# Attention and mixture-of-experts layer: the normalised output turned by a crossbar DMA, and engine orders of their own for each half

## The reference

```
xn  = layernorm(x)
qkv = xn @ W_qkv                      # 32 query heads, 16 key/value heads, 64 wide
p   = softmax(q k^T / 8 + slope_h * (key - query), causal)
s   = concat_heads(p v) @ W_out       # 2048 -> 128
g   = silu(moe(xn))                   # 8 experts, top 2, gelu, 128 -> 512 -> 128
out = x + s * g
```

## Time and profile before

| what | us |
|---|---|
| median of 3 runs | 1367.28 (1366.29 to 1369.7) |
| the profiled execution's own time | 1373.28 |
| its span, first to last instruction | 1370.9 |
| PE / DVE / ACT / POOL busy | 1251.3 / 1103.1 / 891.0 / 833.9 |
| prologue, about | 0 to 90 |
| first half's bodies, about | 90 to 623 |
| experts' stage | 624 to 761 |
| second half's bodies, end of the program | 761 to 1350, 1371 |

### The profile page before, as it was taken

One profiled execution on the slowest core, in us unless ns is written; L12 is line 12 of the kernel. 1 busy time (PEld: TensorE's weight loads), 2 busy tenths in 40 slices (PEclk: granted clock), 3 DMA queues, 4 the chain that ended last, 5 costly groups with the idle time before them and its releaser, 6 DMA issues.

```text
span 1370.9 us, 53673 instructions
## 1 busy us (share of the span) xinstructions
PE 1251.3 (91%) x18202; PEld 934.0 (68%) x18203; DVE 1103.1 (80%) x3404; ACT 891.0 (65%) x1663; POOL 833.9 (61%) x1015
## 2 busy tenths in 40 slices
PE   1589999999999999988999799999999999999992
PEld 0357677777777777767888477766767777667762
DVE  8778788888888888856888688888888888878864
ACT  1367677777777777765666477667666666666662
POOL 7147677777777777780000177776666676666773
PEclk9789999999999999998999899999999999999996
DMA  7223333333333333322222233333333232333322
GB/s 263 89 64 90 77 86 87 87 89 86 84 84 84 84 84 84 84 64 66 80 80 73 70 79 79 78 77 72 71 75 74 69 73 70 72 74 77 77 55 65
DMA packets 113023, 112.37 MB, mean 82 GB/s; under 512 B 17250, under 2 KB 101570, under 8 KB 112324
## 3 DMA queue, kind: packets, MB, share of 16 engines
q1 hardware_dynamic: 108868, 103.18, 30.0%
q0 software_dynamic: 4096, 8.40, 2.0%
HBM read 18.91 MB, written 16.78 MB: 26 GB/s over the span
## 4 chain that ended last, share of the span: by engine, by line
PE 29%; POOL 14%; issue 6%; DVE 5%; ACT 1%; DVEq 0%; POOLq 0%; DMA 0%; SPq 0%; ACTq 0%
POOL h L609 10%; PE ps L631 4%; PE ps L632 4%; PE ps L633 4%; POOL y_now L601 3%; DVE stage L1112 2%; PE ps L728 2%; PE ps L703 2%; PE outs L759 2%; PE ps L732 1%; PE outs L631 1%; PE outs L632 1%; PE outs L633 1%; PE ps L772 1%; DVE mix L1181 1%
## 5 line engine op out<-in xcount | busy, mean ns | idle before, releaser
L609 POOL TENSOR_TENSOR h<-stage 128x512 f16<-128x512 f32 x640 | 646.2, 1038 | 422.1 <-ACT stage L961 384.6
L1112 DVE CUSTOM_DVE_ANT_0 stage<-ps,kmask 128x512 f32<-128x512 f32 (+3 forms) x1024 | 451.7, 488 | 138.4 <-PE ps L703 136.8
L961 ACT ACTIVATE stage<-ps,slope 128x512 f32<-128x512 f32 (+1 forms) x768 | 432.5, 616 | 84.7 <-PE ps L735 81.2
L728 PE MATMUL ps<-q_st,k_st 128*128 128x256 f16 (+3 forms) x1024 | 303.3, 302 | 7.2 <-ACT stage L961 6.3
L759 PE MATMUL outs<-v_sp,stage 128*128 128x65 f16 x2560 | 292.7, 195 | 15.6 <-POOL h L609 12.1
L950 ACT CAST q_st<-ps 1x512 f16<-1x512 f32 x256 | 147.9, 578 | 219.9 <-PE ps L711 218.4
L761 PE MATMUL outs<-v_sp,stage 128*128 128x64 f16 x2560 | 289.8, 194 | 0.0
L763 PE MATMUL outs<-v_sp,h 128*128 128x65 f16 x2560 | 288.9, 193 | 0.0
L759 PEld LDWEIGHTS outs<-v_sp,stage 128*128 128x128 bf16 x2560 | 234.5, 98 | 70.1 <-POOL h L609 33.2
L761 PEld LDWEIGHTS outs<-v_sp,stage 128*128 128x128 bf16 x2560 | 237.5, 98 | 0.0
L763 PEld LDWEIGHTS outs<-v_sp,h 128*128 128x128 f16 x2560 | 237.4, 99 | 0.0
(11 more groups left out here) (192 smaller groups left out, 2852.3 us busy)
## 6 DMA issues: line engine op xcount, KB each, us to landing
q_st<-q_raw SPq DMA_DIRECT2D x256, 128.0 KB, 2.4
k_st<-k_raw SPq DMA_DIRECT2D x128, 128.0 KB, 2.2
q_st<-q_raw SPq DMA_DIRECT2D x256, 64.0 KB, 2.0
k_st<-k_raw SPq DMA_DIRECT2D x128, 64.0 KB, 2.0
stage<-slot_x SPq DMA_DIRECT2D x40, 128.0 KB, 2.0
slot_y<-stage SPq DMA_DIRECT2D x40, 128.0 KB, 1.7
slot_x<-att SPq DMA_DIRECT2D x2, 2048.0 KB, 8.7
wx_raw<-in_L_ffn_w SPq DMA_DIRECT2D x64, 64.0 KB, 1.8
```

Source lines behind the costliest of these rows:

```text
L609: pool.tensor_tensor(t_lo[r], t_p[r], upper(t_p[r]), ALU.subtract).then_inc(s[f"lo{u % NG}"], 1)
L728: pe.matmul(d, k[:, 0, at], q[:, 0, seen], start=True, stop=False, skip_group_check=True)
L961: e = act.activation(t_p[r][:, c0:c1], S_ps[u % 2][:, c0:c1], ACT.Exp, scale=slope[:, bass.ds(pair_index(n) * 2 * SLOTS + sl * 2 + h, 1)])
L1112: ins = dve.tensor_tensor_reduce(junk[h][:, c0:c0 + w], M_ps[h][:, c0:c0 + w], kmask[:, SEQ - w:SEQ], 1.0, -3e38, ALU.add, ALU.max, mx[sl] ...
```

## The change

The A task no longer uses PE. ACT and DVE split a_sb (SBUF, fp32) into a new 16-bit buffer `a16` of 128 x 1024 (512 high columns, then 512 low), and SP turns the whole buffer with one crossbar DMA for each slot and body into `aT`, high and low together. `project` waits for that DMA instead of for `al`. A leaves the G banks. `a16` lies in the stage buffer where the experts' stage has its inputs and outputs, so SP waits for all transposes before the first expert load and ACT waits for the last expert store before the second half's main windows. `ORDER` and `G_USERS` become one set for each half, with the sends and fetches one window later (I and D at -2), A at -1 on DVE and SP, and one more window at the end of each half.

```diff
-    [("Q1", 1), ("A1", -1), ("O0", -1), ("K0", 2), ("A0", 0)],
-    [("V0", 1), ("Q0", 2)],
+    [   # the same for both halves
+        [("V0", 1), ("O0", -1)],
+        [("Q0", 1), ("Q1", 1), ("K0", 2)],
+    ],
...
+ORDER = [   # the second half's list; the first half's differs in places
+        "PE": [
+            ("P6", -1), ("Q0", 1), ("S0", 0), ("P7", -1), ("M5", 0), ("S1", 0), ("P8", -1), ("S2", 0), ("C1", 0),
+            ("S3", 0), ("P9", -1), ("V0", 1), ("M0", 1), ("Q1", 1), ("S4", 0), ("P0", 0), ("M1", 1), ("S5", 0),
+            ("S6", 0), ("P1", 0), ("P2", 0), ("M2", 1), ("S7", 0), ("S8", 0), ("P3", 0), ("C0", 1), ("P4", 0),
+            ("S9", 0), ("K0", 2), ("M3", 1), ("P5", 0), ("O0", -1), ("M4", 1),
+        ],
+        "DVE": [
+            ("O0", -2), ("B5", 0), ("A0", -1), ("Q0", 1), ("N1", -1), ("B0", 1), ("A1", -1), ("B1", 1), ("B2", 1),
+            ("F0", -2), ("F1", -2), ("Q1", 1), ("N0", 0), ("V0", 1), ("B3", 1), ("K0", 2), ("B4", 1),
+        ],
+        "POOL": [
+            ("I1", -2), ("L6", -1), ("D0", -2), ("L7", -1), ("L8", -1), ("L9", -1), ("D1", -2), ("L0", 0),
+            ("L1", 0), ("L2", 0), ("L3", 0), ("L4", 0), ("I0", -1), ("L5", 0),
+        ],
+        "SP": [   # first half: K1 +1, A0 -1, A1 -1, Q0 +1, W0 +2, Q1 +1, K0 +2
+            ("K1", 0), ("Q0", 0), ("K0", 1), ("Q1", 0), ("A0", -1), ("A1", -1),
+        ],
...
+        aT = [h_flat[:, s * 2 * SEQ:(s + 1) * 2 * SEQ] for s in range(SLOTS)]
+        a16 = [piece(8 + s).bitcast(F16) for s in range(SLOTS)]
...
+            def turn_out(n, _, sl):
+                sp.wait_ge(s[f"al{sl}"], n + 1)
+                need(sp, "op", n)
+                sp.dma_start_transpose(aT[sl].rearrange("p (t q) -> p t q", q=P), a16[sl]).then_inc(s[f"ta{sl}"], 16)
...
-                need(pe, f"nrm{sl}", n + 1)
-                bank_free(n, f"A{sl}")
-                for t in range(QT):
-                    mm = pe.transpose(bank_of[f"A{sl}"][:, t * P:(t + 1) * P], a_sb[sl][:, t, :], ident[:, :])
...
-                    need(pe, f"al{sl}", n + 1)
+                    need(pe, f"ta{sl}", (n + 1) * 16)
...
-                act.wait_ge(s[f"ta{sl}"], n + 1)
-                need(act, "op", n)
-                act.copy(aT_hi[sl], bank_of[f"A{sl}"][:, :]).then_inc(s[f"ah{sl}"], 1)
+                act.wait_ge(s[f"nrm{sl}"], n + 1)
+                need(act, f"ta{sl}", n * 16)
+                act.copy(a16[sl][:, 0:SEQ], a_sb[sl].rearrange("p t c -> p (t c)")).then_inc(s[f"ah{sl}"], 1)
...
-                dve.tensor_tensor(aT_lo[sl], bank_of[f"A{sl}"][:, :], aT_hi[sl], ALU.subtract)\
+                dve.tensor_tensor(a16[sl][:, SEQ:2 * SEQ], a_sb[sl].rearrange("p t c -> p (t c)"),
+                                  a16[sl][:, 0:SEQ], ALU.subtract).then_inc(s[f"al{sl}"], 1)
```

More of the change, by code:

```diff
@@ L194, in build @@
         h_flat = h_hi[:, :, :, :].rearrange("p r a b -> p (r a b)")
-        aT_hi = [h_flat[:, s * SEQ:(s + 1) * SEQ] for s in range(SLOTS)]
-        aT_lo = [h_flat[:, (SLOTS + s) * SEQ:(SLOTS + s + 1) * SEQ] for s in range(SLOTS)]
+        aT = [h_flat[:, s * 2 * SEQ:(s + 1) * 2 * SEQ] for s in range(SLOTS)]
+        aT_hi, aT_lo = ([m[:, part * SEQ:(part + 1) * SEQ] for m in aT] for part in range(2))
         flat = stage[:, :, :].rearrange("p a b -> p (a b)")
@@ L261, in one_window @@
         def one_window(engine_name, tasks, w, lo, hi, phase):
-            for name, off in ORDER[engine_name]:
+            for name, off in ORDER[lo // HALF][engine_name]:
                 n = w + off
@@ L290, in run_bodies @@
                     one_window(engine_name, tasks, i_ * UNROLL + c, lo, hi, c)
-            for w in range(end, hi + 1):
+            for w in range(end, hi + 2):
                 one_window(engine_name, tasks, w, lo, hi, w)
@@ L335, in build, with bank_of @@
         M_ps, S_ps, O_ps, G_ps = ps[0:2], ps[2:4], ps[4:6], ps[6:8]
-        bank_of = {name: G_ps[b] for b, users in enumerate(G_USERS) for name, _ in users}
+        def bank_of(name):
+            users_of = G_USERS[bodies_of_half[0] // HALF]
+            return next(G_ps[b] for b, users in enumerate(users_of) if name in [user for user, _ in users])
         def bank_free(n, name):
-            users = next(users for users in G_USERS if name in [user for user, _ in users])
+            users = next(users for users in G_USERS[bodies_of_half[0] // HALF] if name in [user for user, _ in users])
             i = [user for user, _ in users].index(name)
@@ L355, in v_bank @@
         def v_bank():
[L356 removed]
+            return bank_of("V0")[:, :].rearrange("p (t c) -> p t c", t=QT)
         def kv_head(n, sl):
@@ L448, in _ @@
             sp.wait_ge(s["sent"], 2 * NT * 16)
+            for sl in range(SLOTS):
+                sp.wait_ge(s[f"ta{sl}"], HALF * 16)
             for b in range(4):
@@ L671, in keys @@
                 tok = bass.ds(batch_index(n) * SEQ, SEQ)
-                three(bank_of["K0"][:, :], wk_hi[:, w], wk_lo[:, w], xT_hi[:, tok], xT_lo[:, tok])\
+                three(bank_of("K0")[:, :], wk_hi[:, w], wk_lo[:, w], xT_hi[:, tok], xT_lo[:, tok])\
                     .then_inc(s["kmm"], 1)
@@ L927, in k_hi_part @@
                     need(act, f"kst{sl}", n * 32)
-                act.activation(k_raw[:, 0, :], bank_of["K0"][:, :], ACT.Copy, scale=1.0 / WS)\
+                act.activation(k_raw[:, 0, :], bank_of("K0")[:, :], ACT.Copy, scale=1.0 / WS)\
                    .then_inc(s["kh"], 1)
@@ L1020, in _ @@
             enter_bodies("ACT", tasks, HALF, BODIES)
+            for r in range(2):
+                act.wait_ge(s[f"ystore{r}"], NBLK // 2 * 16)
             run_bodies(act, "ACT", tasks, HALF, BODIES)
```

76 lines of the change are left out of this document (43 added, 33 removed), and 10 rows, old and new, of the table ORDER.

## The result

The changed kernel takes 1389.97 us (median of 4 runs, 1388.33 to 1393.26); the kernel before took 1367.34 us beside it. The ratio is 1.0166 [1.0143, 1.0189]: 1.7% slower, where I forecast 4.5% faster, and outside the range.

The account below looks back on a forecast made before the run. It took PE to bound the first half and PE's waits for POOL to slow the second, beside a rough-score loop. 1373.3 - 20 - 47 + 6 = 1312, less 6.0 for the profiled run: 1306 us (-4.5%), range 1266 to 1360.

Parts of the forecast that it names:

- the rival of the slow transpose: PE waits for the transposing DMA in every window; far-end landing 10.5 us, about +115 us, 1480 us; 16%.
- my 0.6 to 2: SP's time to issue each of two more DMAs a body, 0.6 to 2 us, leaving SP free a third of the window.
- my 16.0 and 16.2: Predicted periods per body: 16.0 us in the first half (-20 us), 16.2 us in the second (-47 us).
- the loop of the rough scores: Score banks used in turn by PE, DVE, ACT: 16.0 us a body now, not under 15.4, some 0.3 us hidden reserve.
- a remark in a rival: In the DVE rival: if the lock also falls on the spread (L1119), the gain may go down to -10 us.
- My 16.2 us: Second half's predicted period, down from 17.82 us with POOL's order loosened: -47 us, range -59 to -24.
- The ends: Where the halves end: +3.6 us before the experts and +2.8 us at the second half's end, sum +6 us.
- DVE becomes the bound: Rival: low parts meet POOL at full price, DVE 16.3 us a body, periods 16.4 and 17.0, about 1340 us; 12%.
- my 16% for slower: Chance given to a slower kernel, 0.16, the same as the chance of the slow transpose.
- the third rival: New orders better than credited: PE's small stalls go, only the rough loop holds, 15.4 us both halves, 1267 us; 12%.

Follow-up runs that it names:

- the reductions: Changed kernel with the spread as a one-element DVE reduction and a reduction replacing the output's low part (half left zero); ratio 0.9699, or 0.9577 with Q1's low part earlier.
- after_again: The changed kernel itself, unaltered, measured again in the sitting of the experiments: 1391.4 us, ratio to before 1.0164.
- q1_early_no_holds: Changed kernel, spread and output's low part replaced by reductions (half left zero), Q1's low part ahead of B2 in DVE's second-half list: 1311.3 us, ratio 0.9577.
- spread_reduce: Changed kernel with the spread made a reduction over one element, scale in the maxima, sign in the transpose's identity, same result: 1364.5 us, ratio 0.9955.
- both_reduce: Changed kernel with the spread as a one-element reduction and a reduction in place of the output's low part (half left zero): 1328.8 us, ratio 0.9699.

## Why the prediction was wrong

**What held.** One A task was 0.94 us a body on PE, and with the reductions the first half fell by 0.84 to 0.89 us (16.72 to 15.88 and 15.83). The transposing DMA was taken at 3.5 us and lands in 3.1; it is hidden in the bodies of both stages, at the ends it isn't, and the rival of the slow transpose (16%) is ruled out. Of the two pages of the Trainium skill that the prediction set against each other, the trace agrees with "Advanced Engine Details and Errata", section "X-Bar Transpose (TRN2)" (as fast as regular ones): all eight blocks take 3.1 us, not the estimated 10.5 us of eight times the figure in "VectorE: DVE Perf Modes", section "The three transpose paths". SP needs 1.25 us to issue one, inside my 0.6 to 2. ACT's high part takes 0.62 us (0.58 predicted). PE's waits for POOL's low parts, 25.0 us in 23 bodies, are down to 3.0 us in the whole changed kernel.

**What failed: the price of the held low part, and "That is contained in my 16.0 and 16.2".** This is the step that failed. I gave two low parts 0.8 us a body in the mean and let them vanish in DVE's slack of 1 us. The mean was nearly right, partly by luck: 2 x (1136 - 685) = 0.9 us, but as one hold of 0.8 us every time and one of nothing. Two other things were wrong.

- Where it falls. All of it falls on slot 1's low part, which stands between B0 and B1, inside the loop of the rough scores that I myself had put at 15.4 to 16.0 us with 0.3 us of reserve. Slack of DVE elsewhere in the body is no help. The phases repeat, so the hold isn't a chance but the same in every body. Taking both it and the weights' hold (0.88 us for 0.42) away gives 0.67 us a body in the first half: 16.55 to 15.88.
- What else it lets be held. I left the spread at its size in the kernel before, apart from a remark in a rival. In the new rhythm the spreads of the second half take 0.19, 1.88, 0.19 and 0.61 us in turn over two bodies, 1.06 us a body more than 191 ns each, directly between PE's M and C. Taking this away alone brings the second half from 18.32 to 17.46 us. I also capped a hold at one POOL instruction (1.73 us in all); it can last for a row of them, 1.88 us beside two and 6.64 us beside seven.

**The orders of the second half.** My 16.2 us also took for granted that nothing in the new list binds. The wait of K0 for Q1's low part costs 0.57 us a body even with the reductions in place (17.02 to 16.45), a hold of the expert addition before it included. And POOL's waits for the expert additions, which I expected to vanish, grew: 62.8 us in 23 bodies against 16.7. PE's waits for POOL's low parts are nearly gone all the same, so they seem to cost little; that they matter by packing POOL's rows of low parts behind them is my reading and wasn't tested.

**The ends.** I predicted +6 us for them. By the starts of the accumulates the 15.3 us between the two spans are: +9.1 until the first (105.0 before, 114.2 after: the new order has it later in a window), -7.5 over the 31 intervals of the first half (with the low part of 6.64 us and the wait of 8.2 us for the DMA in them), +7.0 from its last to the second half's first, +6.7 over the 31 intervals there, and nothing behind. The experts begin 1.05 us after the last accumulate in both kernels, not 3 to 4 us later, and their matmuls last 124.5 and 124.6 us; the +7.0 comes after them. The filling of the pipeline, twice 7 to 9 us, was the part I had left out.

**The sum.** From after_again to q1_early_no_holds: spread -27, low part with the weights' hold -36, Q1's entry -17.5 us, together 1391.4 to 1311.3, where I had predicted 1306. The three steps ran on three chips of the same level (before: 1369 to 1371 us), and the last two leave out half of the turned output. So the saving on PE is real, and the changed kernel gives back 80 us through what stands in DVE's list: held instructions and one entry out of place. That 1311 comes so near to 1306 is luck in part: by its accumulates the ends cost 19 us there and not 6, and the first half gave 33 us and not 20. Of the rivals it was "DVE becomes the bound", which I gave 12% and priced as a sum over the body (1340 us); its mechanism was right, its price wrong by a loop and a spread. That DVE could make the kernel slower than before I had not seen; my 16% for slower were all for the DMA.

**What stays open.** Why two of five chips run the kernel before at 1450 us and more, and how much of the first half's period there is the chip's. What the low part would cost alone, without the weights' hold that moves with it. And no kernel that computes everything was more than half a per cent faster than before at the level of 1369 us: spread_reduce (0.9955) is the best. GpSimd's low parts in the second half only, with spread_reduce's first half, weren't tried; 29 x (17.46 - 16.89) = an estimated 17 us less than spread_reduce. How far the rough loop can be shortened isn't known either: in both_reduce's first half PE is busy 377.8 of 380 us, so PE bounds it and the 15.4 us of the third rival were never reached.

## What to carry to other kernels

Moving work from TensorE to a DMA also moves the operand of what follows from PSUM to SBUF; ask of every VectorE instruction downstream whether GpSimd can now hold it, and for how long its instructions run without a gap. Price a hold on the loop in which the instruction stands, not on the engine's busy share, and expect it to fall on the same instruction in every body. Taking one away moves the phases and can set another: judge by the period, not by the instruction that got shorter. Work given to GpSimd makes its rows longer, and with them the holds of whatever stays on VectorE.

## What the runs showed of the hardware that was not expected

- A VectorE instruction with both inputs in SBUF waited for a whole row of GpSimd instructions: 1.88 us beside two (2.05 us of POOL), 5.87 us beside six (6.02 us), 6.64 us beside seven (7.01 us).
- GpSimd is held too where VectorE's instruction comes first: 1566 ns at most, where 1040 is usual. Its mean grew less, from 1038 to 1091 ns.
- A `tensor_scalar` on eight elements with one SBUF input was held as well, up to 2.17 us. A `tensor_reduce` on the same data never was (186 to 197 ns over 128).
- The same subtraction took 685 to 688 ns in the mean whenever one operand was in PSUM, in four kernels, and up to 6.64 us when both were in SBUF.
- A transposing DMA of 256 KB from SBUF to SBUF landed in 3.1 us (3.0 to 4.8) while the DMA engines were busy 0.53 of the time; SyncE was occupied 1.25 us to issue it, where a plain one takes 0.6.
